# A buffer for each half of the output product, and both halves copied ahead of exponential 15

## What is computed

```python
x = x + attn(_layernorm(x))      # 16 heads of 64, causal softmax, layernorm with weights inside
x = x + ffn(_layernorm(x))       # sigmoid encoder, router with 8 experts, top 2, decoder, layernorm

q = einsum('bsd,hde->bshe', x, W_q) + b_q        # k and v likewise
scores = einsum('bqhe,bkhe->bhqk', q, k) * D_HEAD ** -0.5
pattern = softmax(where(causal, scores, -inf), axis=-1)
z = einsum('bhqk,bkhe->bqhe', pattern, v)
attn_out = einsum('bqhe,hed->bqd', z, W_o) + b_o
```

## Time and profile before

| | |
|---|---|
| median of 3 runs | 1162.31 us (1160.6 to 1169.64) |
| the profiled execution | 1161.35 us, span of its instructions 1159.6 us |
| mean granted PE clock | 0.983 of full speed |
| busy, PE / PE weight loads / DVE / ACT / POOL | 89% / 66% / 74% / 64% / 64% |
| 16 DMA engines | 67.9% of their time |

### The profile page before, as it was taken

One profiled execution on the slowest core, in us unless ns is written; L12 is line 12 of the kernel. 1 busy time (PEld: TensorE's weight loads), 2 busy tenths in 40 slices (PEclk: granted clock), 3 DMA queues, 4 the chain that ended last, 5 costly groups with the idle time before them and its releaser, 6 DMA issues.

```text
span 1159.6 us, 51488 instructions
## 1 busy us (share of the span) xinstructions
PE 1033.9 (89%) x19852; PEld 768.7 (66%) x19852; DVE 861.9 (74%) x2047; ACT 739.5 (64%) x1540; POOL 743.9 (64%) x728
## 2 busy tenths in 40 slices
PE   5789999999999999999999999999999978899984
PEld 2567777777777777777777777777777766454542
DVE  7877777777777777777777777777777786357563
ACT  4656666666666666666666666666666655667663
POOL 5786666666666666666666666666666633344544
PEclk8999999999999999999999999999999998899998
DMA  7678877777777777777777777777777773131322
GB/s 172 160 192 210 195 181 186 184 185 186 183 183 187 187 182 188 185 184 184 185 185 184 186 183 184 186 183 186 184 183 186 188 149 76 38 83 47 91 59 51
DMA packets 131599, 188.79 MB, mean 163 GB/s; under 512 B 46576, under 2 KB 57840, under 8 KB 131568
## 3 DMA queue, kind: packets, MB, share of 16 engines
q1 hardware_dynamic: 131568, 188.40, 67.9%
HBM read 133.39 MB, written 21.36 MB: 133 GB/s over the span
## 4 chain that ended last, share of the span: by engine, by line
PE 65%; POOL 13%; issue 8%; DVE 6%; ACT 5%; DMA 1%; POOLq 1%; DVEq 0%; ACTq 0%; SPq 0%
PE ZB L714 27%; PE SPS L697 13%; PE SPS L698 10%; POOL QS L495 6%; PE ZB L687 5%; POOL X L520 3%; POOL QS L493 3%; ACT RAW L1279 2%; ACT OT L1316 1%; PE SPS L849 1%; PE SPS L875 1%; PE ZB L681 1%; PE ZB L890 1%; PE ZB L884 1%; ACT PRL L1299 1%
## 5 line engine op out<-in xcount | busy, mean ns | idle before, releaser
L1018 DVE CUSTOM_DVE_ANT_0 SSB<-SPS,MASK 128x640 f32<-128x640 f32 (+7 forms) x512 | 375.1, 751 | 174.5 <-PE SPS L698 163.6
L714 PE MATMUL ZB<-PTZ,VR 32*64 32x256 f32 (+2 forms) x16384 | 321.5, 294 | 30.9 <-ACT RAW L1279 23.7
L697 PE MATMUL SPS<-KHP,QS 128*128 (+2 forms) x768 | 323.5, 427 | 23.9 <-DVE NM L1018 19.5
L1299 ACT ACTIVATE PRL<-SSB,NM 128x640 f32<-128x640 f32 (+3 forms) x256 | 253.1, 989 | 128.4 <-DVE NM L1018 128.0
L714 PEld LDWEIGHTS ZB<-PTZ,VR 32*64 32x64 f32 x16384 | 271.8, 131 | 77.7 <-issue 63.1
L698 PE MATMUL SPS<-KLP,QS 128*128 (+2 forms) x768 | 259.7, 348 | 0.0
L981 DVE STREAM_TRANSPOSE PTZ<-PRL 128x640 f32<-128x640 f32 (+3 forms) x256 | 257.6, 1026 | 0.0
L1299 ACT ACTIVATE PRS<-SSB,NM 128x128 f32<-128x128 f32 (+3 forms) x256 | 142.6, 558 | 139.8 <-DVE NM L1018 139.5
L697 PEld LDWEIGHTS SPS<-KHP,QS 128*128 128x128 f32 x768 | 145.3, 189 | 99.3 <-issue 45.8
L495 POOL TENSOR_TENSOR QS<-RAW,QS 64x512 fp32r<-64x512 f32 x128 | 165.0, 1289 | 10.3
L514 POOL TENSOR_TENSOR PTZ<-PTZ,RSB 128x512 f32<-128x512 f32 x64 | 81.2, 1291 | 139.6 <-ACT PTZ L1310 139.3
(11 more groups left out here) (170 smaller groups left out, 1053.4 us busy)
## 6 DMA issues: line engine op xcount, KB each, us to landing
VR<-v_scratch SPq DMA_DIRECT2D x256, 256.0 KB, 6.8
KHP<-KHP SPq DMA_DIRECT2D x64, 256.0 KB, 3.2
KLP<-KLP SPq DMA_DIRECT2D x64, 256.0 KB, 3.8
v_scratch<-V SPq DMA_DIRECT2D x32, 512.0 KB, 7.0
RSB<-rcp_scratch SPq DMA_DIRECT2D x64, 256.0 KB, 3.9
XTB<-xt_scratch SPq DMA_DIRECT2D x62, 256.0 KB, 4.4
XW<-xt_scratch SPq DMA_DIRECT2D x30, 512.0 KB, 7.4
VR<-gate_scratch SPq DMA_DIRECT2D x16, 512.0 KB, 5.9
```

The lines of the kernel that those rows point to most:

```text
L697: pe.matmul(SP_[n % 2][:, c0:c0 + wc], q, kh[:, c0:c0 + wc], start=True, stop=False)
L714: last = pe.matmul(ZB[h * DH:(h + 1) * DH, i, kt * TR:QT * TR], VR[rows, j, kt, h * DH:(h + 1) * DH], turned_block(h, kt, j, rows), start= ...
L1018: v.tensor_tensor_reduce(out=SSB[n % 2][:, 0:w], in0=SP_[n % 2][:, 0:w], in1=MASK[:, S - w:S], scale=1.0, scalar=BIG, op0=ALU.add, op1=ALU ...
L1299: act.activation(exps_of(n), SSB[n % 2][:, 0:w], ACT.Exp, bias=NM[:, col:col + 1], scale=-1.0, accum_out=L[:, col:col + 1]).then_inc(exp_d ...
```

## The change

OT gets two halves, `add_out` and `out_of` use half g, and ACT's step copies both halves ahead of exponential 15. The first memset clears both and counts two, so that `out_evac` is one higher than before at any time after it, and the four waits in other places that count it are raised by one. The wait of `out_of(g)` keeps its number: with the count one higher, it now holds until the same half of the step before has been added, where it held until the half just before had.

```diff
-        OT = sb("OT", [P, CH])
+        OT = sb("OT", [P, 2, CH])
...
-            gp.tensor_tensor(xs, xs, OT[:, :].rearrange("p (t d) -> p t d", d=D), ALU.add).then_inc(out_evac, 1)
+            gp.tensor_tensor(xs, xs, OT[:, g, :].rearrange("p (t d) -> p t d", d=D), ALU.add).then_inc(out_evac, 1)
...
-            gp.memset(OT[:, :], 0.0).then_inc(out_evac, 1)
+            gp.memset(OT[:, :, :], 0.0).then_inc(out_evac, 2)
...
-                    gp.wait_ge(out_evac, it * 2)
+                    gp.wait_ge(out_evac, it * 2 + 1)
...
-                    gp.wait_ge(out_evac, it * 2 + 1)
+                    gp.wait_ge(out_evac, it * 2 + 2)
...
-                v.wait_ge(out_evac, (STEPS - HP) * 2 + 1)
+                v.wait_ge(out_evac, (STEPS - HP) * 2 + 2)
...
-                    v.wait_ge(out_evac, STEPS * 2 + 1)
+                    v.wait_ge(out_evac, STEPS * 2 + 2)
...
             act.wait_ge(out_filled, it * 2 + g + 1)
             act.wait_ge(out_evac, it * 2 + g + 1)
-            act.activation(OT[:, :], bank, ACT.Copy).then_inc(out_copied, 1)
+            act.activation(OT[:, g, :], bank, ACT.Copy).then_inc(out_copied, 1)
...
             exps_to(14, 15)
             out_of(0)
+            out_of(1)
             exps_to(15, 16)
-            out_of(1)
```

## The result

The changed kernel takes 1201.2 us in the median (1199.47 to 1208.38), against 1161.45 us for the kernel before in the same comparison: a ratio of 1.034 with a 95% interval of 1.028 to 1.041, so it is about 40 us slower. The forecast was 1204.8 us, in a range of 1172 to 1212.

The account below looks back on a forecast made before the run. The attention steps were taken as bound by a chain through PE, ScalarE and POOL's add and splits. Schedule 0, ends -1.4 and clock falls +44.8 on 1161.35 gave 1204.8 us, range 1172 to 1212.

Parts of the forecast that it names:

- The chain through POOL: Steady steps: copy 0, POOL's add and two splits, then evacuation 3 hold the value products, which start at 530.75 as before.
- The moved wait: PE's 0.93 us saved before qk(2) reappear behind scores(4), where the wait grows from 0.87 to 1.80 us; sum 0.
- Exponential 15: On ScalarE it starts some 0.6 us later behind copy 1, at no cost; without cover 0.6 us a step.
- the cover that was named: VectorE's turn 15 stands behind mask 2, leaving 2.6 us of slack; mask 1 waits behind turn 14 anyway.
- The clock: PE's granted clock falls over the value products in 28 steps, 1.6 us each, 44.8 us; chance 0.68.
- one fall of three similar gaps: PE gaps of 1.8 to 2.04 us in the old profile: clock down at 983.5, up at 79.9 and 994.3.
- the small piece of work between two idle spells: On PE, scores(4) between two waits ahead of the value products was held to tip the clock down, 29 times over.
- Rival 2: PE's clock falls in only some steady steps, half of 29: 1183 us, between 1172 and 1195; chance 0.13.
- The mean granted clock: PE's mean clock over the kernel was to go down from 0.983 to about 0.90.
- The ends: Step 31 gains about 0.3 us and the first feed-forward chunk 1.1 us from earlier copy 1; together -1.4 us.

Follow-up runs that it names:

- splits first alone: Changed kernel with POOL's splits of queries 2 and 3 put ahead of both adds: 1123.0 us, ratio 0.967 to the kernel before.
- filler: Changed kernel with unread 128x512 products on PE behind scores(4) in each step: two gave 1158.07 us, one gave 1162.21 us.
- The wait put back: Changed kernel with one more wait on PE, qk(2) held until ScalarE has evacuated qk(0): 1157.36 us, ratio 0.996 to the kernel before.

## Why the prediction was right, and where it was off

**The chain through POOL** was read rightly. Copy 1 wasn't in it, evacuation 3 still waits for the second split, and splits first alone gave 39 us against the kernel before, with a period of 27.9 us in place of 29.1, which shows that this chain, not the copies, set the period.

**The moved wait.** Forecast 0.93 us earlier and a gap of 1.80 us. Counted from the output products, scores(4) came 1.03 us earlier (6.76 us behind them, 7.79 before), and the gap is 1.86 us. The total forecast for the wait on RAW, near 50 us, was 53.8.

**Exponential 15** costs nothing, with the cover that was named: the two edits of order and buffer apart show it, and the order alone costs 0.2%.

**The clock.** It fell in 28 steps, as forecast, each costing 44.6 / 28 = 1.59 us (forecast 1.6). That the low clock on the value products is what costs the time was rightly seen; that it would be 28 steps and not some was luck as much as reading. What the prediction had to judge by was thin, one fall of three similar gaps, and its own reason, the small piece of work between two idle spells, was a guess from step 31. It set the two gaps that left the clock up apart as standing between long dense runs, but the gap at 983.5, whose clock fell, also had dense work before it: PE's only pause from 974.66 to its start was one of 0.19 us. The runs show that the length of the gap alone does not decide: 1.4 us fell in every step (own halves, old order), 1.0 us behind a filler in none, and 2.7 us in the one-buffer kernel with splits first in only 7 of 29. That a small piece of work between two idle spells tips it was not tested apart from the rest. Rival 2, a fall in some steps, came out in none of the kernels with an early `qk(2)`: it was nearly all steps or none. The mechanism of the loss was shown, by filler and by wait; how the chip decides wasn't.

**The mean granted clock** was forecast as 0.90 and is 0.944. That number did not follow from the forecast's own terms: 28 low stretches of 3.4 us are 95 us of 1199, which at half the clock takes 0.04 off the mean, not 0.08.

**The ends.** In the first chunk copy 1 now waits 0.30 us for PE's product instead of 1.43 us for POOL:

```profile
1034.50 0.60 ACT L1316 ACTIVATE OT<-ZB 128x512 f32<-128x512 f32 x1 [0.30 <-PE ZB L722]
```

The gain of some 1.1 us there fits, but as a part of the whole it can't be told. The 39.1 us by which the span grew are these: the start is 2.7 us shorter (value products of step 2 at 91.1 against 93.8); the steady steps with their 28 falls add 44.4; and what lies behind them is 2.6 us shorter, where the low stretches of the clock stand in other places than before. Start and end together give 5.3 us where the forecast had 1.4, and that, not the steps, is why the profiled execution took 1200.5 and not 1204.8 us. The wait put back, which keeps this gain, is 0.4% faster than the kernel before, 4 us. That is more than 1.4 us; what the remainder is stays open.

## What to carry to other kernels

A wait taken from the busiest engine is worth nothing while another chain ends at the same point: follow what is late next before you count the gain. And when such a wait moves, look at where the engine's idle time gathers; here much the same idle time of TensorE, bunched to 1.86 us in one place where it had been 0.77 and 0.87 us in two, lowered the clock in 28 of 29 rounds and cost 44.6 us, where the wait that was taken away had cost 22.7. A buffer that frees two engines from each other pays when the order of the engine on the critical chain is changed to use it: here the adds could go behind the splits, and only then did it bring 3.3%, and 4.2% with VectorE's turn 15 moved as well.

## What the runs showed of the hardware that I had not expected

The falls settled into the rhythm of the steps. In the changed kernel and in the one with own halves and the old order, once the first fall had come, the period became 30.7 us in both, though their gaps differ by 0.4 us (1.86 and 1.44), and every later step fell. Why the period is the same in both is open. A gap of 2.7 us between two dense runs, in the one-buffer kernel with splits first, left the clock up in 22 of 29 steps; this is one of the seven behind which it fell:

```profile
583.37 1.02 PE L681 MATMUL ZB<-XTB,WQK 128*128 128x512 f32 x2
587.08 1.13 PE L681 MATMUL ZB<-XTB,WQK 128*128 128x512 f32 x2 [2.69 <-ACT OT L1316]
```

So the length of the longest gap did not tell which kernel would lose its clock. And one of the edits that gave the 40 us back was a product that nobody reads: useless work on the critical engine, which fills 0.86 us of the gap in each step (1.86 to 1.00).
